# One launch of four attention blocks: large loads behind the first key copies, two short warm-up matmuls, and the third batch's last feed-forward beside the last batch's closing chain

## The reference, cut to what matters

```
L0: x = softmax(q k^T) v @ Wo + bo + x          # cross attention to the context, 20 heads of 8
L1, L3 (each):
    h = ln(x);  x = attn(h, h) @ o1 + b + x      # self attention, 20 heads of 8
    h = ln(x);  x = attn(h, ctx) @ o2 + b + x    # cross attention, 20 heads of 8
    h = ln(x);  a, g = split(h @ ff_w1 + ff_b1)  # 160 -> 2 x 640
    x = (a * gelu(g)) @ ff_w2 + ff_b2 + x        # 640 -> 160
L2: out = mha(x Wq, enc Wk, enc Wv)              # 8 heads of 20, 508 context rows
    c = mha(ca_q1, x, x); c = mha(c Wq, ca Wk_ca, ca Wv_ca)   # last 4 context rows
    x = (out + c) @ Wout + b_out + x
```

## Time and profile before

| | us |
|---|---|
| median of three runs | 921.88 |
| lowest, highest | 921.34, 934.77 |
| the profiled execution | 923.25 |
| its span, first to last instruction | 921.3 |
| TensorE busy | 880.2 (matmul records 7810) |
| VectorE, ScalarE, GpSimd busy | 669.9, 654.7, 55.3 |
| mean granted TensorE clock | 0.998 |

### The profile page before, as it was taken

The page is one execution under the profiler, slowest core; times in us unless marked ns, Lnnn a source line. Parts: engine busy times, 40 slices in busy tenths (PEclk is TensorE's granted clock), DMA queues, the critical chain, the costliest instruction groups (busy, mean ns, idle before and its releaser), DMA issues.

```text
span 921.3 us, 21210 instructions
## 1 busy us (share of the span) xinstructions
PE 880.2 (96%) x7810; PEld 594.2 (64%) x7810; DVE 669.9 (73%) x1607; ACT 654.7 (71%) x1423; POOL 55.3 (6%) x92
## 2 busy tenths in 40 slices
PE   8999999999999999999999999999999999999987
PEld 6656565666666577676667776665676666766655
DVE  3978878878788876657566667776777898686822
ACT  7677786877777777667777576676777777776652
POOL 2000000000000000000000000000000000000100
PEclk9999999999999999999999999999999999999999
DMA  8111121111111201001000300001102111111100
GB/s 292 43 36 36 36 47 24 24 29 24 27 44 33 47 22 26 19 18 36 13 1 2 124 3 2 22 11 28 30 19 47 36 32 28 31 36 24 31 9 7
DMA packets 25964, 32.21 MB, mean 35 GB/s; under 512 B 9220, under 2 KB 17416, under 8 KB 25608
## 3 DMA queue, kind: packets, MB, share of 16 engines
q1 hardware_dynamic: 25864, 30.86, 13.1%
HBM read 9.21 MB, written 0.66 MB: 11 GB/s over the span
## 4 chain that ended last, share of the span: by engine, by line
PE 79%; DVE 8%; ACT 8%; issue 4%; ACTq 0%; DVEq 0%
PE pv_ps L1010 17%; PE bank_ps L952 12%; PE bank_ps L972 11%; PE bank_ps L928 8%; PE bank_ps L929 7%; DVE mx L1428 5%; PE bank_ps L1057 5%; PE bank_ps L986 4%; ACT probs L1259 3%; PE bank_ps L1037 3%; PE bank_ps L1130 3%; PE bank_ps L1118 2%; PE bank_ps L1174 2%; ACT oT L1268 1%; PE bank_ps L1076 1%
## 5 line engine op out<-in xcount | busy, mean ns | idle before, releaser
L1428 DVE TENSOR_REDUCE mx<-bank_ps 128x1 f32<-128x512 f32 (+3 forms) x720 | 452.1, 682 | 91.0 <-PE bank_ps L972 89.6
L1259 ACT ACTIVATE probs<-bank_ps 128x512 f32<-128x512 f32 x736 | 380.9, 601 | 116.7 <-PE bank_ps L952 115.2
L1010 PE MATMUL pv_ps<-probs,v 128*9 128x256 f32 (+2 forms) x2944 | 199.3, 376 | 5.4 <-ACT probs L1259 2.3
L952 PE MATMUL bank_ps<-qT,ring 64*128 64x256 f32 x1280 | 171.0, 303 | 2.5 <-DVE gate L1515 1.0
L972 PE MATMUL bank_ps<-ring,qT 64*128 64x512 f32 (+1 forms) x800 | 168.4, 393 | 2.4 <-ACT kdense L1310 1.1
L952 PEld LDWEIGHTS bank_ps<-qT,ring 64*128 64x128 f32 x1280 | 128.6, 185 | 62.7 <-issue 22.3
L972 PEld LDWEIGHTS bank_ps<-ring,qT 64*128 64x128 f32 x800 | 87.3, 184 | 43.2 <-issue 19.6
L1010 PEld LDWEIGHTS pv_ps<-probs,v 128*9 128x9 f32 (+2 forms) x2944 | 57.4, 90 | 76.4 <-issue 22.7
L1310 ACT ACTIVATE kdense<-bank_ps 128x512 fp32r<-128x512 f32 (+2 forms) x116 | 58.3, 556 | 22.2 <-PE bank_ps L1057 21.8
L1234 ACT ACTIVATE ks<-bank_ps 128x320 fp32r<-128x320 f32 x80 | 35.7, 447 | 42.5 <-PE bank_ps L929 22.1
L1452 DVE TENSOR_TENSOR qT<-bank_ps,qT 128x256 fp32r<-128x256 f32 (+1 forms) x108 | 47.0, 436 | 23.6 <-PE bank_ps L986 23.2
(11 more groups left out here) (178 smaller groups left out, 1037.1 us busy)
## 6 DMA issues: line engine op xcount, KB each, us to landing
ring<-kdense SPq DMA_DIRECT2D x240, 64.0 KB, 2.0
ring<-kdense SPq DMA_DIRECT2D x160, 32.0 KB, 1.9
wb<-in_w_blk SPq DMA_DIRECT2D x2, 2240.0 KB, 8.4
wd<-in_w_down SPq DMA_DIRECT2D x2, 400.0 KB, 8.5
x<-in_x SPq DMA_DIRECT2D x4, 160.0 KB, 4.5
bias<-in_bias SPq DMA_DIRECT2D x1, 640.0 KB
out_rows<-x SPq DMA_DIRECT2D x4, 160.0 KB, 1.9
gate<-in_ctx SPq DMA_DIRECT2D x3, 192.0 KB, 4.8
```

Source lines behind the costliest of these rows:

```text
L952: mm = pe.matmul(bank[0:kr, i * a["nq"]:(i + 1) * a["nq"]], key_op(n, h)[:, c * P:c * P + kr], query_rows(u, b, h), start=True, stop=True)
L1010: mm = pe.matmul(pv_ps[32 * j:32 * j + a["dh"] + 1, 0:a["nq"]], v, probs[0:kr, s % N_P, i * a["nq"]:(i + 1) * a["nq"]], start=(c == 0), st ...
L1259: nc.scalar.activation(probs[0:kr, s % N_P, 0:w], bank[0:kr, 0:w], ACT.Exp, scale=float(a["dh"]) ** -0.5).then_inc(free, 1)
L1428: nc.vector.tensor_reduce(mx[b][0:rows, t, heads[0]:heads[-1] + 1:heads[-1] - heads[0] or 1], bank[0:rows, 0:a["hpm"] * a["nk"]].rearrange ...
```

## The change

1. Start: `WARM_UP` goes from four matmuls of 512 columns to two of 320. The transfer of `wc` is split: only the 320 columns of the first attention come first. The other 640 columns, the remaining main weights, biases, tables, last rows of the context and `block_weights(0)` are issued by `later_weights()`, behind the sixteen ring copies of the first four groups (`FIRST_KEYS = 4`).
2. SP's wait for `ca_q` stands at the step `low` of `ca_q`, not at `ca_q`.
3. End: `keep_clock` and its five matmuls are gone. The feed-forward of batch 2 (`B - 2`) joins `LAST_FEEDS`, with gelu chunk by chunk. Its steps are no longer placed in the stream of the last attention but form a fifth stage that opens once the last slot of scores and `o_proj` of batch 2 are placed. The plan is then made anew: the first 2831 of its 2995 steps are as before.

```diff
--- before.py
+++ after.py
@@ -57,10 +57,12 @@
     6: dict(kind="cross", H=20, dh=8, sr=32, nq=SQ, nk=SK, hps=2, hpm=1),
 }
 PHASES = [(0,), (1,), (2,), (4, 3), (5,), (6,)]
-WARM_UP = 4
-LAST_WARM = 4
+WARM_UP = 2
+FIRST_KEYS = 4
+LAST_SLOTS = 0
 LAST_FEED = ("ff3", B - 1)
-N_CONST = 8
+LAST_FEEDS = [("ff3", B - 2), LAST_FEED]
+N_CONST = 9
 N_BANK = 7
 N_P = 8
 RING = 4
@@ -171,14 +173,14 @@
     return [normed(u, b) + queries(u, b), ctx_keys(u, b)]
 
 
-def behind(ph, b):
+def behind(ph, b, part=0):
 
     def output(u):
         return [("x_bias", u, b)] + [("o_nat", u, b, i) for i in range(3)] + [("o_tr", u, b), ("o_proj", u, b)]
 
     def feed(tag):
         first = [("ln", tag, b), ("x_bias", tag, b), ("norm", tag, b), ("h_tr", tag, b)]
-        if (tag, b) == LAST_FEED:
+        if (tag, b) in LAST_FEEDS:
             return first + [(kind, tag, b, i) for i in range(3) for kind in ("ff_g", "ff_a")] + [("ff_o", tag, b)]
         return (first + [("ff_g", tag, b, i) for i in range(3)] + [("gelu", tag, b)]
                 + [("ff_a", tag, b, i) for i in range(3)] + [("ff_o", tag, b)])
@@ -186,6 +188,8 @@
     if ph == 3:
         return [("x_bias", 3, b), ("o_nat", 3, b, 0), ("o_tr", 3, b), ("c_o", b), ("o_proj", 3, b)]
     steps = output(PHASES[ph][0])
+    if (ph, b) == (5, B - 2):
+        return steps if part == 0 else feed("ff3") + [("store", b)]
     return steps + feed("ff1") if ph == 2 else steps + feed("ff3") + [("store", b)] if ph == 5 else steps
 
 
@@ -236,7 +240,7 @@
 
     total = len(slots)
     lead = M_LEAD + FIRST_W + K_LEAD + 1
-    stages = [[], [], [], []]
+    stages = [[], [], [], [], []]
 
     def spread(lo, hi, steps):
         for i, step in enumerate(steps):
@@ -255,6 +259,9 @@
             stages[2].append(([("oev", last[4])], [last_rows(b)]))
         spread(span[k][1] + PV_LAG + 1 - BG_LEAD, until, behind(ph, b))
         stages[3 if k == len(PHASES) * B - 1 else 2].append(([("oev", last[PHASES[ph][-1]])], [behind(ph, b)]))
+    beside = behind(len(PHASES) - 1, B - 2, 1)
+    spread(total, total + 2 * TAIL, beside)
+    stages[4].append(([("st", total - 1 - LAST_SLOTS), ("o_proj", PHASES[-1][0], B - 2)], [beside]))
     for s in range(total):
         put(s, -1, ("st", s))
     order, place = simulate(quads, slots, due, stages)
@@ -868,21 +875,25 @@
                 context_in(sp, 0)
                 sp.dma_start(ident[:, :], io["ident"]).then_inc(s_ident, 16)
                 rows_in(sp, 0)
-                sp.dma_start(wc[:, :], io["w_ctx"]).then_inc(s_wc, 16)
+                kv = W_CTX[0][1]
+                sp.dma_start(wc[:, 0:kv], io["w_ctx"][:, 0:kv]).then_inc(s_wc, 16)
                 first = W_MAIN["q0"][1]
                 sp.dma_start(wm[:, :, 0:first], io["w_main"][:, :, 0:first]).then_inc(s_wq, 16)
                 for b in range(1, B):
                     context_in(sp, b)
                     rows_in(sp, b)
-                sp.dma_start(wm[:, :, first:], io["w_main"][:, :, first:]).then_inc(s_w, 16)
-                sp.dma_start(bias[:, :], io["bias"].broadcast_to([P, 8 * D])).then_inc(s_w, 16)
-                for dst, src in ((lncols, "lncols"), (kmask, "kmask")):
-                    sp.dma_start(dst[:, :, :], io[src]).then_inc(s_w, 16)
-                for dst, src in ((cols, "cols"), (wqca, "w_qca"), (spread, "spread"), (vmask, "vmask")):
-                    sp.dma_start(dst[:, :], io[src]).then_inc(s_w, 16)
-                for b in range(2):
-                    last_rows_in(b)
-                block_weights(0)
+                def later_weights():
+                    sp.dma_start(wc[:, kv:], io["w_ctx"][:, kv:]).then_inc(s_w, 16)
+                    sp.dma_start(wm[:, :, first:], io["w_main"][:, :, first:]).then_inc(s_w, 16)
+                    sp.dma_start(bias[:, :], io["bias"].broadcast_to([P, 8 * D])).then_inc(s_w, 16)
+                    for dst, src in ((lncols, "lncols"), (kmask, "kmask")):
+                        sp.dma_start(dst[:, :, :], io[src]).then_inc(s_w, 16)
+                    for dst, src in ((cols, "cols"), (wqca, "w_qca"), (spread, "spread"), (vmask, "vmask")):
+                        sp.dma_start(dst[:, :], io[src]).then_inc(s_w, 16)
+                    for b in range(2):
+                        last_rows_in(b)
+                    block_weights(0)
+
                 sp.wait_ge(s_zero, 1)
                 for step in order:
                     if step[0] == "kdma":
@@ -900,14 +911,16 @@
                             rows = slice(32 * j, 32 * j + 32)
                             sp.dma_start(ring[rows, at, j % 2, 0:a["nk"]].bitcast(F32),
                                          kdense[b][rows, qd, 0:a["nk"]].bitcast(F32)).then_inc(ring_in[at], 16)
+                        if n == FIRST_KEYS - 1:
+                            later_weights()
                     elif step == ("ff_o", "ff1", B - 1):
 
                         taken(sp, step)
                         block_weights(1)
-                    elif step[0] == "ca_q" and step[1] + 2 < B:
-
-                        taken(sp, step)
-                        last_rows_in(step[1] + 2)
+                    elif step[0] == "low" and step[1][0] == "ca_q" and step[1][1] + 2 < B:
+
+                        taken(sp, step[1])
+                        last_rows_in(step[1][1] + 2)
                     elif step[0] == "store":
                         b = step[1]
                         taken(sp, ("ff_o", "ff3", b))
@@ -928,14 +941,9 @@
                     pe.matmul(out, lhs[:, 0, :], rhs[:, 0, :], start=True, stop=False)
                     return pe.matmul(out, lhs[:, 1, :], rhs[:, 1, :], start=False, stop=True)
 
-                def keep_clock(n):
-
-                    for _ in range(n):
-                        pe.matmul(pv_ps[:, :], ident[:, :], probs[:, N_P - 1, :], start=True, stop=True)
-
                 pe.wait_ge(s_warm, 1)
                 for _ in range(WARM_UP):
-                    pe.matmul(bank_ps[0][:, :], probs[:, 0, 0:P], probs[:, 0, :], start=True, stop=True)
+                    pe.matmul(bank_ps[0][:, 0:320], probs[:, 0, 0:P], probs[:, 0, 0:320], start=True, stop=True)
                 for step in order:
                     kind = step[0]
                     if kind == "st":
@@ -1063,8 +1071,6 @@
 
                         _, tag, b = step
                         bank, full = take(step)
-                        if (tag, b) == LAST_FEED:
-                            keep_clock(LAST_WARM)
                         src = natural(tag, b) if tag in LNS else x[b]
                         if tag in LNS:
                             pe.wait_ge(S["xn_ready"], value["xn_ready", ("norm", tag, b)])
@@ -1132,8 +1138,6 @@
                     elif kind == "o_tr":
                         _, u, b = step
                         bank, full = take(step)
-                        if ends(u, b):
-                            keep_clock(1)
                         for i in range(1 if u == 3 else 3):
                             taken(pe, ("o_nat", u, b, i))
                         nat = out_natural(u, b)
@@ -1356,7 +1360,7 @@
                         for k, m in enumerate(range(2 * i, min(2 * i + 2, FC))):
                             c = (0 if tag == "ff1" else 2 * FC) + FC + m
                             ins = nc.scalar.activation(gate_of(tag, b)[:, m, :], bank[:, k * SQ:(k + 1) * SQ],
-                                                       ACT.Gelu if (tag, b) == LAST_FEED else ACT.Identity, bias=cols[:, c:c + 1])
+                                                       ACT.Gelu if (tag, b) in LAST_FEEDS else ACT.Identity, bias=cols[:, c:c + 1])
                         ins.then_inc(free, 1)
                     elif kind == "gelu":
                         _, tag, b = step
```

## The result

The changed kernel takes **920.43 us** in the median of 22 runs (917.66 to 926.51), the kernel before 928.31 (920.94 to 934.77, 22 runs, the three ahead of the prediction among them). The ratio is **0.9932, with a 95% interval of 0.9912 to 0.9952**: a gain of 0.7% that is small but outside what chance gives. (It isn't the quotient of the two medians, which would be 0.9915.) The profiled execution of the changed kernel took 917.91 us with a span of 916.1, where that of before took 923.25 with 921.3.

A forecast was written before the change was run, and what follows sets the result against it. PE, busy 96% of the span, was taken as the bound. Start -1.9 and third feed-forward -3.9 (-12.1 in the attention, +8.2 in the closing chain) sum to -5.8: 917.4, or 916 us by the median; eight-in-ten range 911 to 921.5.

The forecast's parts named there:

- (a): Closing chain, before the copy of the last sums: ACT must take the first gelu first, +3.0 us.
- Start, early work and ring wait: Start: first key projection 1.8 us earlier, and PE's 1.07 us wait for ring copies goes.
- Start, clock: Start: first pieces may run at 1.2 GHz after the shorter warm-up, taken as +1.0 us.
- clock stays low at the start: Rival, start: it costs +1.6 us instead of -1.9, giving 919.5; chance 0.13.
- Large loads, later: After the start: large loads behind sixteen ring copies land near 39 us, before they are needed; cost 0.
- Third feed-forward out of the last attention: Last batch's attention: PE is relieved of 12.0 us of the third batch's feed-forward; the replay gives -12.1 us.
- (b): Closing chain, transposes to the merged rows: one step of 1.73 us replaces the dummy, -0.3 us.
- (c): Closing chain, to the output projection: 1.73 us of work where PE waited 0.8, +0.9 us.
- (d): Closing chain, from the output projection's end to the last norm's transposes: third batch's work stands ahead, +4.6 us.
- last attention not PE's: Rival, last attention: the removed 12 us come back as only 7, giving 921; chance 0.10.
- closing chain goes cold: Rival, end: without dummies the clock falls and the last feed-forward costs another 11.6 us, 927.6; chance 0.06.
- More comes back: Rival: the gap of (d) is covered, or the earlier clock drop doesn't recur, 911 to 913; chance 0.11.

The follow-up runs named there:

- experiment 3: The change, with SyncE issuing the stores of batches 0 and 1 behind the next group's ring copies: 916.24 us, ratio 0.9886.
- experiment 1: The kernel before with only the change's start (two short warm-up matmuls, large loads behind sixteen ring copies): 921.07 us, ratio 0.9941.
- experiment 4: Experiment 3 with four steps of the last batch's closing chain moved ahead of pieces of the third batch's feed-forward: 918.24 us, ratio 0.9893.
- experiment 9: Experiment 3 run again, same edit to the change: 917.06 us, ratio 0.9925.
- experiment 10: Experiment 4 run again, same edit: 915.68 us, ratio 0.9889.
- experiment 11: Experiment 9 with five short dummy matmuls of 256 columns in the closing chain: 918.78 us, ratio 0.9931.
- experiment 12: Experiment 10 with four short dummy matmuls of 256 columns in the closing chain: 914.99 us, ratio 0.9881.
- Experiment 6: The kernel before with only the short warm-up, two matmuls of 320 columns, loads where they were: 927.49 us, ratio 1.0030.
- Experiment 8: The kernel before without its five dummy matmuls in the closing chain: 930.94 us, ratio 1.0038.

## Why the prediction was right and wrong

Four stretches of the profiled execution, in us against the kernel before. "The gelu" is again that of batch 1's last feed-forward, at 839.30 before and 835.10 in the change:

| stretch | forecast | the change | experiment 3 |
|---|---|---|---|
| to the first maximum | -1.9 | -2.8 | -2.8 |
| from there to the gelu | 0 | -1.4 | -1.5 |
| from there to the last copy of sums, with (a) | -9.1 | **-5.6** | -9.8 |
| from there to the last addition | +5.2 | +4.6 | +6.3 |
| sum | -5.8 | -5.2 | -7.8 |

The second row is no work of the change but the fall of the clock in the earlier trace rows, which did not recur: the change is 2.8 us ahead at 52 us, 4.4 at 90 and still 4.2 at 835.

- *The size.* Forecast -5.8 us of 921.88, that is a ratio of 0.9937; measured 0.9932. That they agree is in good part luck. By the trace the work of the change is worth 3.8 us and not 5.8, which fits the 4 us of the runs at a high clock; the start brought 0.9 more than forecast, the end (the last two stretches) 1.0 instead of 3.9, and a fall of the clock that didn't recur fills the gap. The mechanism was right for the start, for PE's relief in the attention and for the closing chain, and it lacked one queue (below). The cases, too, were weighed by a bound of 2% ("about what a measurement of this kernel can tell"). That was wrong: the interval over 22 runs is 0.2% to either side. The 0.96 on "within" followed from that bound, not from the sum; by the sum it should have lain on a small gain.
- *Start, early work and ring wait:* forecast -1.8 and -1.07, measured -2.1 and -0.7. Right.
- *Start, clock:* forecast +1.0, "between nothing and 4.5". In this profile nothing, by the projection's 1.32. But it is a toss: with the change's warm-up and loads the profiles of experiments 1, 3, 4, 9 and 10 show it at full pace, those of 11 and 12 at half, with the first maximum at 22.88 and 22.41 instead of 21.1 to 21.4. (Experiment 6, with the same warm-up and the old loads, was at half pace too.) So it is some 1.3 us in some runs, not 1.0 in each. The Trainium skill ("TensorE: Matmul & The Clock Gate", Part 1) says that at a kernel's start the number of slow matmuls varies from run to run; these rows agree. The rival "clock stays low at the start" is thus true in part of the runs: there is that half pace, but the start still brings 1.3 to 1.7 us and doesn't cost 1.6.
- *Large loads, later:* the ring copies near 40 us landed in 4.1 us in the median and 5.4 at most (2.6 and 3.0 before), where the text said "wrong if later than 4". No pause of PE came of it: its pauses from 34 to 64 us are 0.22 and 0.69, the same two as before. The cost of 0 stands, its margin was smaller than said. So does the 0 for SP's moved wait: SP waits 36.5 us there in all, before 36.2.
- *The step that failed:* **"Third feed-forward out of the last attention ... -12.1"**, with SP's queue taken as unchanged (only the wait at `low` was costed, "0"). The replay's rows are of PE, ACT and DVE; no term had the wait of SP at a store, and so that of PE for the ring copies behind it, nor the fall of the clock behind such a pause. With (a) inside, the stretch to the last copy should have given -12.1 + 3.0 = -9.1; it gave -5.6. The missing 3.5 are the store: the new plan put it ahead of the copies of group 113, SP waited 15.4 us in front of them, PE 2.85, and the clock fell. Experiment 3 moves only the stores of batches 0 and 1 and gets -9.8, 4.2 more. With the store behind these copies the replay was good to 0.7 us.
- *The closing chain:* (b) to (e) sum to +5.2, measured +4.6: (b) -0.3, (c) +0.8, (d) +4.1 instead of 4.6. Right. The check in the text, "33 us" and "that copy 14 us earlier", contradicted its own working, since (a) lies before the copy; it should have read 30 and 11 (measured 29.4 and 9.8). The pause before the last norm's transposes is 1.22 us where 1.8 was said.
- *Rival "last attention not PE's":* from 870 to 880 us ACT is busy 9.24 of 10 in the changed kernel and PE 9.19, so they now tie (rows below), and in experiment 3 ACT leads there, 9.09 to 7.71; but with the store moved all of the 12 us comes back (-9.8 with (a)'s +3.0 in it). A loss of the size that it foresaw came from SP.
- *Rival "closing chain goes cold":* not in the profile of the change (0.43 a pair), but in those of experiments 3 and 9, and then for 1.7 and 1.6 us, not 11.6; the clock came back within four pairs. Experiment 8 shows that its premise was true: without the dummies, and without real work for them, the clock fell. Why the fall came in both profiles of experiment 3's order and in none of the two of experiment 4's isn't settled.
- *More comes back:* the drop of the earlier trace rows didn't recur in the profile, but 911 to 913 was not reached by the change. It was in reach: 911.51 in experiment 4, 912.45 and 912.86 in experiment 10, at a high clock.

The rows for the rival that ACT takes over, windows of the changed kernel:

```profile
870.00:880.00 10.00, 9.19 (x125) 5.71 (x124) 5.43 (x14) 9.24 (x21) 2.59 (x4) 1.00 0.01 2
880.00:890.00 10.00, 8.38 (x59) 6.71 (x52) 2.28 (x9) 4.37 (x10) 0.00 (x0) 1.00 0.00 0
```

Not tried: holding the store back by more than one group, and a warm-up long enough to lift the clock before 6.75 us in every run.

## What to carry to other kernels

When a planner makes its order anew, list the order of every queue that waits in it, that of SP too: a store that waits for its data holds up each prefetch behind it, and the cost shows up on another engine labelled "issue". Put such a store behind the next prefetch. Here that took 4.2 us off the stretch it lies in, in both profiles, and another 2 us off the whole (915.9 against 918.0, medians of the runs at a high clock), half as much as the whole change had (from 922); the ratios, 0.9886 and 0.9925 against 0.9932, show it only once. And two edits at one place (shorter warm-up, loads out of the way) can be worth more together than apart: price the pair, with the wait that each alone would run into.

## What the runs showed of the hardware that was not expected

**The granted clock falls behind short pauses in some runs and not in others, and that is most of the spread between runs.** The kernel before took 921.2 to 922.7 us in its 14 runs with a mean clock of 1.000, about 926 at 0.994 (25 runs) and 931.9 to 934.0 at 0.987 (4 runs). Several of the places are the same in many profiles. PE's timeline of the kernel before near 377 us:

```profile
377.69 1.06 PE L1130 MATMUL bank_ps<-ident,oT 128*128 128x128 f32 x8 [1.41 <-ACT oT L1268]
```

and of experiment 10 at the same step, with its window:

```profile
373.34 1.88 PE L1155 MATMUL bank_ps<-ident,oT 128*128 128x128 f32 x8 [1.41 <-ACT oT L1291]
```

```profile
374.00:376.00 2.00, 2.00 (x8) 1.23 (x7) 1.12 (x5) 0.00 (x0) 0.00 (x0) 0.50 0.00 0
```

The same pause of 1.41 us, once without and once with the fall. All fourteen profiles have this pause; the clock fell there or right behind in seven. Other falls came behind pauses of 1.69 (experiment 4, 639 us), 0.55 (experiment 1, 89.5 us) and 0.69 us (before, 54.5 us, the fall in the earlier trace rows), in the last two after PE had taken up work again at full pace. Each of these pauses stands in other profiles without a fall. PE is busy 1.00 while the clock is low, so the busy share of a slow stretch doesn't tell why it is slow.

**The windows name 1.00 where the pace is half.** In the first 10 us the clock column reads 1.00 in every profile, and a run's mean clock doesn't hold this loss either (experiment 11's profile has 1.000). Only the durations show it, here the same step in experiments 9 and 11, whose code is alike up to there:

```profile
6.75 1.31 PE L1055 MATMUL bank_ps<-wc,ctxT 128*128 128x320 f32 x4 [1.16 <-ACT ctxT L1288]
```

```profile
6.75 2.47 PE L1059 MATMUL bank_ps<-wc,ctxT 128*128 128x320 f32 x4 [0.88 <-ACT ctxT L1298]
```
